# First loads of the layers moved into the attention stage, later weights issued by SyncE, sequence loops written out

## What is computed

```python
x = L0_attn_x                                   # (4, 1024, 256)
xn = _layernorm(x, axis=-1)
x = x + _L0_attn_ref(xn, ...) + _L0_ffn_ref(xn, ...)

# _L0_attn_ref: 16 heads of 64
xn = rms_norm(x, gamma, dim)
q, k, v = split(xn @ W_qkv)
out = sliding_window_attention(q, k, v, 64) * sigmoid(xn @ W_gates + b_gates)
return out @ W_out

# _L0_ffn_ref: two layers, 8 heads of 64, HID = 682
h = shift_token(x)
q, k, v = split(h @ wqkv)
q, k = rotary_xpos(l2norm(q) * q_scale, l2norm(k) * k_scale)
x = x + local_attention(q, k, v) @ wo
h = layernorm(shift_token(x)) * ln_g + ln_b
a, g = split(h @ w1 + b1)
x = x + (a * gelu(g)) @ w2 + b2
```

## Time and profile before

| what | us |
|---|---|
| median of 3 runs | 2125.22 |
| lowest and highest | 2119.74 and 2127.86 |
| the profiled execution, its own time | 2126.16 |
| its span, first to last instruction | 2124.4 |

### The profile page before, as it was taken

One profiled execution on the slowest core, in us unless ns is written; L12 is line 12 of the kernel. 1 busy time (PEld: TensorE's weight loads), 2 busy tenths in 40 slices (PEclk: granted clock), 3 DMA queues, 4 the chain that ended last, 5 costly groups with the idle time before them and its releaser, 6 DMA issues.

```text
span 2124.4 us, 46932 instructions
## 1 busy us (share of the span) xinstructions
PE 1918.1 (90%) x15184; PEld 1585.8 (75%) x15184; DVE 1329.3 (63%) x4117; ACT 1404.3 (66%) x3934; POOL 963.6 (45%) x1311
## 2 busy tenths in 40 slices
PE   5998999899998479999989999996999998999998
PEld 3777787677777358778777787885877877778777
DVE  4543543444443167768767777785776876777765
ACT  4885977778778155756747657665575674765764
POOL 2532442433334155626527447353463662654732
PEclk9999999999999689999999999998999999999999
DMA  3321231213212600110101101204011010110110
GB/s 122 96 86 67 70 104 52 94 64 93 88 51 81 221 31 11 43 45 11 41 17 41 41 6 49 102 6 147 21 44 54 21 43 26 40 51 16 39 33 26
DMA packets 120637, 121.75 MB, mean 57 GB/s; under 512 B 27172, under 2 KB 100916, under 8 KB 120372
## 3 DMA queue, kind: packets, MB, share of 16 engines
q1 hardware_dynamic: 108848, 100.89, 15.0%
q10 hardware_dynamic: 11524, 17.57, 2.4%
HBM read 72.78 MB, written 37.25 MB: 52 GB/s over the span
## 4 chain that ended last, share of the span: by engine, by line
PE 29%; DVE 14%; issue 10%; ACT 8%; POOL 3%; ACTq 2%; DVEq 0%; POOLq 0%
PE f_bank L1283 10%; PE f_scores L1420 4%; PE f_scores L1358 4%; ACT f_prob L1517 4%; PE f_bank L1406 4%; PE f_bank L1366 3%; DVE f_gu L1670 3%; PE f_bank L1330 2%; DVE f_x_tok L1656 2%; PE f_o_bank L1381 2%; ACT f_u L1537 2%; DVE f_x_tok L1662 1%; DVE f_sin_part L1576 1%; DVE f_rstd L1649 1%; POOL f_prob L1236 1%
## 5 line engine op out<-in xcount | busy, mean ns | idle before, releaser
L1236 POOL TENSOR_SCALAR f_prob<-f_prob,f_row_inv 128x256 f32<-128x256 f32 x512 | 264.5, 538 | 366.2 <-DVE f_row_inv L1616 366.2
L522 POOL TENSOR_SCALAR a_prob<-a_prob,a_row_inv,a_gate 128x128 f32<-128x128 f32 x512 | 225.9, 464 | 418.2 <-DVE a_row_inv L849 418.2
L1283 PE MATMUL f_bank<-f_wqkv,f_actT 128*128 128x512 f32 x1152 | 302.5, 407 | 14.8 <-DVE f_actT L1559 14.8
L1406 PE MATMUL f_bank<-f_hT,f_w 128*128 128x256 f32 x2112 | 275.3, 285 | 7.3 <-DVE f_gu L1670 7.3
L1406 PEld LDWEIGHTS f_bank<-f_hT,f_w 128*128 128x128 f32 x2112 | 261.0, 189 | 14.0 <-DVE f_gu L1670 10.4
L1517 ACT ACTIVATE f_prob<-f_scores,f_neg_max 128x256 f32<-128x256 f32 x512 | 236.2, 488 | 40.0 <-DVE f_neg_max L1608 39.8
L1283 PEld LDWEIGHTS f_bank<-f_wqkv,f_actT 128*128 128x128 f32 x1152 | 209.3, 191 | 63.6 <-issue 17.8
L1608 DVE CUSTOM_DVE_ANT_0 f_scores<-f_scores,f_mask 128x256 f32<-128x256 f32 x512 | 200.2, 454 | 37.2 <-PE f_scores L1358 33.9
L1212 POOL TENSOR_TENSOR f_norm<-f_norm,f_minus_half 128x16 f32<-128x16 f32 x64 | 199.1, 3112 | 47.7 <-DVE f_norm L1568 45.2
L748 ACT ACTIVATE a_prob<-a_scores,a_neg_max 128x128 f32<-128x128 f32 x512 | 179.9, 391 | 40.9 <-DVE a_neg_max L840 40.6
L1537 ACT ACTIVATE f_u<-f_gu 128x256 fp32r<-128x256 f32 x192 | 80.2, 418 | 179.0 <-DVE f_gu L1670 179.0
(11 more groups left out here) (124 smaller groups left out, 3918.4 us busy)
## 6 DMA issues: line engine op xcount, KB each, us to landing
split_weights<-a_hi_lo SPq DMA_DIRECT2D x16, 512.0 KB, 2.8
f_x_next<-states SPq DMA_DIRECT2D x32, 256.0 KB, 2.9
f_tables<-scaled_tables SPq DMA_DIRECT2D x16, 512.0 KB, 5.7
f_x<-states SPq DMA_DIRECT2D x16, 512.0 KB, 4.8
split_weights<-a_hi_lo SPq DMA_DIRECT2D x12, 682.0 KB, 4.2
f_w<-split_weights ACTq DMA_DIRECT2D x4, 1280.0 KB, 13.1
a_x_tok<-in_x SPq DMA_DIRECT2D x8, 512.0 KB, 4.2
states<-a_x_tok SPq DMA_DIRECT2D x8, 512.0 KB, 4.4
```

Of the source, the lines that this page charges most:

```text
L522: last = nc.gpsimd.tensor_scalar(part, part, row_inv[:, a % 2, head, t:t + 1], gate[:, half, t, h:h + 1], ALU.mult, ALU.mult)
L1236: last = nc.gpsimd.tensor_scalar(part, part, row_inv[:, a % 2, head, t:t + 1], 1.0, ALU.mult, ALU.mult)
L1283: last = nc.tensor.matmul(out, lhs(c, a), rhs(c, b), start=(i == 0), stop=(i == len(order) - 1))
L1406: mm = nc.tensor.matmul(out[:, which * PART:(which + 1) * PART], w1[:, wp, c, col:col + P], hT[:, hp, c, columns_of(a // FH)], start=(i == ...
```

## The change

The two stages share some tiles now, which are allocated around both (`Kept`): the identity, the rows `y_tok` (the layers' `x_tok`), `x_next`, `tables`, and `weights`. That last one is the first stage's Q and K projection weights, and after the last Q/K projection it takes the layers' `wqkv` and `wo`. V's weights of the first stage have a tile of their own.

- In the first stage's last sequence SP issues `first_rows` (x rows and tables) at the step `("project_v", 15)`, and ScalarE issues the three parts of `wqkv` after its copies of `("project_qk", 15)`. The layers' SP waits for the rows at its start. The layers no longer load the identity.
- The first stage's SP doesn't wait for the last `attended` stores at its end; the layers' SP does, behind its first loads.
- `load_others` is issued by SP: for layer 0 behind the second x transfer, and for layer 1 at a new step `("load_others", 0)` of sequence 4, which stands behind `load_x1` and ahead of `load_tables`.
- `wqkv` is loaded in three parts (Q, K, V) with a semaphore each instead of two.
- All loops over sequences are Python loops, so the code is written out.

```diff
+def first_rows(sp, kept, states, tables_in):
+    for ahead, cols in ((1, slice(0, P)), (0, slice(P, D))):
+        sp.dma_start(kept.x_next[:, :, cols], tokens_of(states, 0, 0, ahead=ahead)[:, :, cols]).then_inc(kept.rows_loaded, 16)
+    sp.dma_start(kept.tables[:], tables_in[0]).then_inc(kept.rows_loaded, 16)
+
+def load_projections(act, kept, weights_in):
+    source = weights_in.rearrange("t (c p) n -> p t c n", p=P)
+    for i, loaded in enumerate(kept.weights_loaded):
+        cols = slice(i * F_INNER, (i + 1) * F_INNER)
+        act.dma_start(layer_projections(kept.weights)[:, :, :, cols].bitcast(F32), source[:, :, :, cols]).then_inc(loaded, 16)
...
@@ attention_phase, SP
             sp.dma_start(states[:, 0, :], zero_rows[:]).then_inc(zero_rows_stored, 16)
+            sp.wait_ge(zero_rows_stored, 16)
...
+                    elif step == ("project_v", TILES * BLOCKS - 1) and is_last(it, BATCH):
+                        sp.wait_ge(normed_stored.sem, normed_stored.upto(it, -1))
+                        sp.wait_ge(tables_stored.sem, tables_stored.upto(it, -1))
+                        first_rows(sp, kept, states, tables_out)
...
-            with sp.Fori(0, BATCH - 1) as it:
+            for it in range(0, BATCH - 1):
                 iteration(it, steps)
             iteration(BATCH - 1, last)
-            for each in (y_stored, normed_stored, weights_stored, tables_stored, rows_stored):
+            for each in (normed_stored, weights_stored, tables_stored, rows_stored):
                 sp.wait_ge(each.sem, each.end())
-            sp.wait_ge(zero_rows_stored, 16)
...
@@ attention_phase, ScalarE
                         take_whole(it, kind, a)
+                        if (kind, a) == ("project_qk", PAIRS * BLOCKS - 1) and is_last(it, BATCH):
+                            act.wait_ge(weights_stored.sem, weights_stored.upto(it - 1, -1))
+                            load_projections(act, kept, split_weights[0][0])
...
@@ ORDER
-         ("scores", 2), ("transpose", 0), ("softmax", 2), ("scores", 3), ("weigh", 2), ("weigh", 3), ("load_x1", 0), ("transpose", 1),
-         ("softmax", 3), ("load_tables", 0), ("project_qk", 0), ("rope", 0), ("scores", 4), ("values", 0), ("values", 1), ("take_o", 0),
+         ("scores", 2), ("transpose", 0), ("softmax", 2), ("scores", 3), ("weigh", 2), ("weigh", 3), ("load_x1", 0), ("load_others", 0),
+         ("transpose", 1), ("softmax", 3), ("load_tables", 0), ("project_qk", 0), ("rope", 0), ("scores", 4), ("values", 0), ("values", 1),
...
@@ layers_phase, SP
-            load_rows(0, 0)
-            sp.dma_start(ident[:], identity).then_inc(ident_loaded, 16)
-            load_tables(None, HALVES - 1, 0)
-
+            sp.wait_ge(kept.rows_loaded, 16 * FIRST_ROWS)
+            sp.sem_inc(x_loaded.sem, 32)
+            sp.sem_inc(tables_loaded.sem, 16)
             sp.dma_start(mask[:], masks.rearrange("s p k -> p s k")).then_inc(consts_loaded, 16)
             sp.wait_ge(filled.sem, filled.past(None, ("transpose_x", HALVES - 1), CT - 1))
             load_rows(0, HALVES - 1)
+            sp.wait_ge(pad_zeroed, 1)
+            load_others(0)
             sp.wait_ge(zeroed, 1)
+            sp.wait_ge(kept.attended_stored, attended_end)
...
+                    elif kind == "load_others":
+                        if isinstance(it, int) and it == BATCH:
+                            for each in (filled, ln_ready, x1_biased, gelued, emptied, downed):
+                                sp.wait_ge(each.sem, each.upto(it, -1))
+                            load_others(layer)
...
@@ layers_phase, TensorE
                     if a % TILES == 0:
-                        pe.wait_ge(qk_weights, loads(1, layer))
+                        pe.wait_ge(kept.weights_loaded[QUERY], loads(1, layer))
+                        pe.sem_inc(pe_carried, 1)
                         pe.wait_ge(emptied.sem, emptied.past(it, ("transpose_x", a // TILES), CT - 1))
                     for which in (QUERY, KEY):
+                        if which == KEY and a % TILES == 0:
+                            pe.wait_ge(kept.weights_loaded[KEY], loads(1, layer))
+                            pe.sem_inc(pe_carried, 1)
...
@@ layers_phase, ScalarE
-            load_wqkv(0)
-            act.wait_ge(pad_zeroed, 1)
-            load_others(0)
             for kind, a in before:
...
-                        load_wqkv(next_layer)
+                        load_projections(act, kept, wqkv_in[next_layer])
...
-            with act.Fori(0, BATCH - 1) as it:
+            for it in range(0, BATCH - 1):
                 iteration(it, steps, 0, 0)
             iteration(BATCH - 1, steps, 0, 1)
-            for each in (filled, ln_ready, x1_biased, gelued, emptied, downed):
-                act.wait_ge(each.sem, each.upto(BATCH, -1))
-            load_others(1)
-            with act.Fori(BATCH, SEQUENCES - 1) as it:
+            for it in range(BATCH, SEQUENCES - 1):
                 iteration(it, steps, 1, 1)
             iteration(SEQUENCES - 1, last, 1, 1)
```

More of the change, by code:

```diff
@@ L13 @@
 from contextlib import ExitStack
+from dataclasses import dataclass
 import numpy as np
@@ L281, in attention_phase @@
         y_loaded = count("y_loaded", {"load_y": 1}, unit=16)
-        y_stored = count("y_stored", {"load_y": 1}, unit=16, credit=1)
+        y_stored = Count(kept.attended_stored, BATCH, before, steps, last, {"load_y": 1}, 16, 1)
         weights_loaded = count("weights_loaded", {"weights_in": 1}, unit=16)
@@ L660, in iteration @@
                         gates_back(it, a)
-            with pe.Fori(0, BATCH - 1) as it:
+            for it in range(0, BATCH - 1):
                 iteration(it, steps)
@@ L876, in iteration @@
                                                 ALU.subtract).then_inc(weights_split.sem, 1)
-            with dve.Fori(0, BATCH - 1) as it:
+            for it in range(0, BATCH - 1):
                 iteration(it, steps)
             iteration(BATCH - 1, last)
+        return y_stored.end()
 PER_CHUNK = {"load_x": 1, "load_tables": 1, "load_x1": 1, "scores": 8, "softmax": 8, "weigh": 8, "transpose": 8, "values": 8,
@@ L919, in layers_phase @@
         rows = sb("rows", [P, ROWS])
-        ident = sb("ident", [P, P])
+        ident, x_tok, x_next, tables = kept.ident, kept.y_tok, kept.x_next, kept.tables
         mask = sb("mask", [P, 2, 2 * P])
@@ L936, in layers_phase @@
         prob = sb("prob", [P, 2, 2, 2, 2 * P])
-        tables = sb("tables", [P, 2, 2, TILES, DH])
         qk_tok = sb("qk_tok", [P, TILES, 2, F_INNER])
@@ L1133, in load_tables, with load_others @@
                 sp.dma_start(tables[:], tables_in[layer * HALVES + half]).then_inc(tables_loaded.sem, 16)
-            load_rows(0, 0)
-            sp.dma_start(ident[:], identity).then_inc(ident_loaded, 16)
-            load_tables(None, HALVES - 1, 0)
+            def load_others(layer):
+                sp.dma_start(wo.bitcast(F32), wo_in[layer].rearrange("t (c p) n -> p t c n", p=P)).then_inc(wo_loaded, 16)
+                sp.dma_start(rows[:], rows_in[layer]).then_inc(rows_loaded, 16)
+                weights, half = w1_in[layer].rearrange("t (c p) n -> p t c n", p=P), REST // 2
+                for which in (0, 1):
+                    c0, rest = which * HID, REST + which * P // 2
+                    for place, cols in ((slice(which * half, (which + 1) * half), slice(c0, c0 + half)),
+                                        (slice(rest, rest + HL), slice(c0 + half, c0 + HID))):
+                        sp.dma_start(w1[:, :, :, place].bitcast(F32), weights[:, :, :, cols]).then_inc(w1_loaded, 16)
+                weights, full = w2_in[layer], (FH - 1) * HT
+                for part in (HI, LO):
+                    sp.dma_start(w2[:, part, 0:FH - 1, :].bitcast(F32), weights[part, 0:full, :].rearrange("(j p) n -> p j n", p=HT)).then_inc(w2_loaded, 16)
+                sp.dma_start(w2[0:HL, :, FH - 1, :].bitcast(F32), weights[:, full:HID, :].rearrange("t p n -> p t n")).then_inc(w2_loaded, 16)
+            sp.wait_ge(kept.rows_loaded, 16 * FIRST_ROWS)
+            sp.sem_inc(x_loaded.sem, 32)
+            sp.sem_inc(tables_loaded.sem, 16)
             sp.dma_start(mask[:], masks.rearrange("s p k -> p s k")).then_inc(consts_loaded, 16)
@@ L1260, in iteration @@
                             pool.sem_inc(attended_added.sem, 1)
-            with pool.Fori(0, BATCH) as it:
+            for it in range(0, BATCH):
                 iteration(it, steps, 0)
-            with pool.Fori(BATCH, SEQUENCES - 1) as it:
+            for it in range(BATCH, SEQUENCES - 1):
                 iteration(it, steps, 1)
@@ L1319, in prepare @@
                 elif kind == "project_v":
-                    pe.wait_ge(v_weights, loads(1, layer))
+                    pe.wait_ge(kept.weights_loaded[2], loads(1, layer))
                     out = take_bank(it, filled.number(it, (kind, a)))
```

120 lines of the change are left out of this document (61 added, 59 removed).

## The result

The changed kernel takes 2062.81 us (median of 4 runs, 2060.92 to 2063.74) against 2123.99 us for the kernel before (4 runs beside it). The ratio is 0.9711, with a 95% interval of 0.969 to 0.9732. The profiled execution took 2062.13 us, its span is 2060.3 us, 64.1 us less than before.

A forecast was written before the change was run, and what follows sets the result against it. TensorE, busy nine tenths of the span, was taken to lose time at the change of stage, sequence boundaries and change of layer. Gains 12.1 + 19.2 + 25.8 + 4.0 = 61.1 us from 2126.16 gave 2065, range 2050 to 2080.

The forecast's parts named there:

- Part 1: Sequence boundaries: writing out the loops removes jumps, 12.1 us in the first stage and 19.2 in the layers.
- Part 2: Change of stage: first loads issued in the first stage bring the first projection from 729.82 to 704.0, gaining 25.8 us.
- The sign given for this part: Layers' start: no DMA issue of ScalarE, projections 6 to 7 us after the first stage's last store is issued.
- The cover of SP's long issue: Layers' start: layer-0 weight issues hold SP until some 718, its next duty is near 744; hidden, 25 us of cover.
- Part 3: Change of layer: weights on SP free ScalarE, but VectorE waits 9.8 us for tables; gain 4.0 us, between 2 and 16.2.
- the upper bound: Change of layer: tables in at 1470.4 at the latest, from 1448.5 plus 16.2 us of issue and 5.7 of landing.
- (a): Change of layer: tables in time or VectorE's wait absorbed, so that place gains 16.2 us, total 2053; chance 0.14.
- (b): Loops written out gain nothing, since straight code stalls for instructions as a jump does: 2096; chance 0.10.
- (c): Whole kernel: straight code stalls at each of 137 instruction-queue refills; slower than before, 2202 at 1 us each; chance 0.04.
- (d): End of first stage: first loads delay the last weight quarter, its split and store; at most 11 us, 2076; chance 0.10.

The follow-up runs named there:

- the reordered kernel: Changed kernel with SP's step for the layer-1 weights moved from ahead of the tables' load to behind it, nothing else: 2050.38 us, ratio 0.965.

## Why the prediction was right

The forecast was 2065, 61.1 us below the profiled execution; the profiled execution gave 64.0 and the median is 2062.8.

**Part 1, the loops: 31.3 forecast.** The two jumping boundaries of the first stage give 12.1 and the six of the layers 19.3, as forecast. Of the 12.1 only 10.9 reach the ends of the two sequences (they are 5.2 and 5.7 us shorter): 1.2 us is given back inside sequence 1, for a reason that no run was made to find. Taking the part alone gave 31.3, undoing it 31.2 to 34. The step that carried it was to compare boundaries with and without a jump in one trace, whole distances and not the engines' stalls; a sum of the stalls would have counted several that run side by side. (The sequences between the boundaries of layer 0 in the kernel before are 148.9 us each, and not 148.9 to 149.0; nothing hangs on it.)

**Part 2, the change of stage: 25.8 forecast.** The trace gives 27.7 less the 0.9 that the end of the first stage lost, 26.7. The transposes began 1.1 us after the last store's issue and not 1.7, ScalarE's copy 0.7 after them and not 1.0, and ScalarE's issues cost 1.1 in place of 1.5. The sign given for this part, projections 6 to 7 us behind the last store, was wrong: they come 3.8 us behind it. It counted ScalarE's 1.5 us, which fall ahead of that store, and the start was 1 us sooner. From the first projection to the first product it then took 10.5 us and not 9.9 as before, so of the 28.3 us gained at the projections 27.7 are left. The cover of SP's long issue held: its last one begins at 703.97 and holds it 1.88 us, and its next duty, an x transfer, comes only at 738.05.

**Part 3, the change of layer: 4.0 forecast**, from 9.8 us of waiting and 2.5 us of lower clock. It is 11.2 us of waiting (27.02 - 15.82), and 1.6 us that sequence 4 takes longer than sequence 5 (152.71 against 151.08). The net is 183.5 - 179.7 = 3.8. The terms were off by about one us each and cancelled, which is luck: the forecast let 20 us pass from the first weight's issue until the tables are in, and it was 21.9, from 1396.10 to 1418.01. SP issued the table 20.3 us after the last addition, within the 21.8 of the upper bound, and it took 6.7 us to land where that bound had 5.7. That a queue is consumed in order, which the Trainium skill states ("DMA: Bandwidth & Descriptors", queues, rings and completion order), agrees with the trace here, where the table, issued behind the nine at 1411.33, lands at 1418.0, and the DMA engines then fall idle (0.01 in the stretch behind); that it decides the place is shown by the kernel in which only the order differs.

**The rivals.** (a), no give-back, fell with the 11.12 us on the row; it is what the reordered kernel reaches, 2050 against the 2053 worked out for it. (b) and (c) fell with the six boundaries of 15.82 and the sequences of unchanged length: straight code showed no stall for its instructions, also not while the DMA engines were full of weights. Of the 137 packets that (c) counted on q8 the straight code still has 122, and 0.45 us for each would be 55 us. (d) gave 1.1 us by the issues, and nothing by the transfers.

**What was not forecast** is the 2.2 us of the last sequence, most of the 3 us by which the forecast fell short. Its code and its waits are the same; it had two stretches of 6.8 us at the lower clock in the kernel before and has one now. In the other kernels of this study that sequence took 136.1 to 138.3 us, so this is where the stretches fall and no gain of the change.

## What to carry to other kernels

A long list of DMA issues belongs to an engine that has nothing else due, and within that engine's queue the transfer that is needed first goes first: moving the issues freed ScalarE, but behind the weights the tables left 3.8 us of it, and ahead of them 16.6. Cost a loop by the distance between two fixed instructions at a boundary that jumps and at one that falls through, both of which one trace may hold. Write out loops of which each iteration is long, as here with 165 us and few iterations: the loop registers and branch instructions cost nothing that shows, the taken branches cost 3 to 6 us a boundary where all engines jump.

## What the runs showed of the hardware

- Behind a taken branch VectorE's stream stands for 2.62 us where it alone jumps, and one engine is enough to lengthen the boundary: TensorE's alone brings it to the 20.3 us that all bring, 4.5 above the 15.82 without. TensorE's own timeline there, in the kernel in which it alone jumps, has two idle times that end with its own issue, 3.2 us in all, and the granted clock over the 12 us behind has a mean of 0.72 against the 1.00 of the changed kernel; how the 4.5 divide between the two was not measured. A branch that is not taken costs nothing that shows (15.85). The last row below is a stretch, with the columns of the earlier trace rows.

```profile
907.92 2.58 PE L1492 MATMUL f_scores<-f_w,f_u 128*128 128x256 f32 x18
912.50 1.88 PE L1430 MATMUL f_scores<-f_kT,f_q 64*128 64x256 f32 x9 [2.00 <-issue]
915.62 2.08 PE L1430 MATMUL f_scores<-f_kT,f_q 64*128 64x256 f32 x7 [1.24 <-issue]
...
911.00:923.00 12.00, 8.67 (x44) 5.87 (x46) 5.46 (x24) 5.57 (x20) 3.25 (x8) 0.72 0.24 73
```

- A DMA issue is not free when many transfers are under way: nine issues of 5.6 MB hold the issuing engine for 15 to 17 us, on ScalarE (15.9 at the change of stage, 16.9 at the change of layer) as on SP (15.1 at either, and 17.2 with the tables first). That is about the time in which the data move: at the 344 GB/s of the 17.2 us on SP, 5.6 MB take 16 us. Three issues of 1 MB with nothing before them on ScalarE's queue hold it 1.50.
- Where a short stretch of lower clock falls differs from kernel to kernel for the same instructions. The last five result tiles of the first stage come as before in half of the fourteen traces and 1.4 to 2.0 us later in the others; with the tables first, for one, the grant is 0.50 from 680.2 to 683.6 us. Among the kernels in which nothing at the change of stage was put back, it then takes 13.4 to 13.6 us in four and 14.6 in the one with all loops back; with the tiles in time it takes 14.7 or 14.8 us, but 12.07 where VectorE alone jumps and the grant stays at 1.00 throughout. Single us in one trace should be laid against this.
